# Softmax attention: maxima over 1024 keys in one pass, exponentials by single heads, the value product in one run a step

## The reference

```python
q = (x @ Wq).reshape(b, s, N_HEADS, D_K)
kk = (x @ Wk).reshape(b, s, N_KV, D_K)
v = (x @ Wv).reshape(b, s, N_KV, D_K)
...
scores = jnp.einsum('bqkgd,btkd->bkgqt', q, kk) * inv_sqrt_dk
attn = jax.nn.softmax(scores, axis=-1)
out = jnp.einsum('bkgqt,btkd->bqkgd', attn, v)
```

## Time and profile before

| | |
|---|---|
| time, median of 3 runs (lowest, highest) | 5175.65 us (5169.24, 5177.06) |
| the profiled execution: time, span | 5170.96 us, 5169.3 us |
| busy share of the span: TensorE, VectorE, ScalarE, GpSimd | 81%, 66%, 41%, 39% |
| granted TensorE clock, mean of the span | 0.916 |

### The profile page before, as it was taken

One profiled execution on the slowest core, in us unless ns is written; L12 is line 12 of the kernel. 1 busy time (PEld: TensorE's weight loads), 2 busy tenths in 40 slices (PEclk: granted clock), 3 DMA queues, 4 the chain that ended last, 5 costly groups with the idle time before them and its releaser, 6 DMA issues. The chain is left out here.

```text
span 5169.3 us, 79734 instructions
## 1 busy us (share of the span) xinstructions
PE 4208.5 (81%) x24362; PEld 2099.4 (41%) x24362; DVE 3391.5 (66%) x7610; ACT 2094.7 (41%) x3092; POOL 2028.3 (39%) x2141
## 2 busy tenths in 40 slices
PE   1548999999999999997588627787787797999999
PEld 0122333333333333333466514344344354666665
DVE  6838888888888888884455464454454555666665
ACT  1014555555555556555455402222222133333333
POOL 0300022212222222222344426656666663666665
PEclk9968999999999999998799858888888898999999
DMA  2951111111111111110322200000000001000000
GB/s 84 384 176 24 25 33 33 33 33 33 33 33 33 34 34 35 34 37 11 115 87 88 76 10 20 25 14 23 20 16 24 19 10 33 21 19 18 19 20 20
DMA packets 132918, 237.92 MB, mean 46 GB/s; under 512 B 27552, under 2 KB 32872, under 8 KB 132520
## 3 DMA queue, kind: packets, MB, share of 16 engines
q1 hardware_dynamic: 115656, 200.51, 14.5%
q0 software_dynamic: 16384, 33.59, 2.3%
q10 hardware_dynamic: 576, 0.02, 0.0%
HBM read 89.74 MB, written 144.31 MB: 45 GB/s over the span
## 5 line engine op out<-in xcount | busy, mean ns | idle before, releaser
L917 DVE TENSOR_REDUCE b_halfmax<-b_ps_m 128x1 f32<-128x512 f32 x2048 | 1342.0, 685 | 300.1 <-PE b_ps_m L1182 293.5
L1150 ACT ACTIVATE b_probs<-b_ps_s 128x1024 f32<-128x1024 f32 x1024 | 993.5, 1019 | 623.9 <-PE b_ps_s L1194 618.4
L1182 PE MATMUL b_ps_m<-b_ks,b_qs 96*128 96x512 bf16 x2048 | 827.7, 405 | 177.5 <-DVE b_halfmax L917 134.0
L1209 PE MATMUL b_ps_o<-b_probs,b_vs 128*32 128x256 f32 x8192 | 664.3, 401 | 0.6 <-ACT b_probs L1150 0.6
L1891 POOL TENSOR_TENSOR e_act_lo<-e_act,e_act_hi 128x512 fp32r<-128x512 f32 x384 | 519.2, 1352 | 348.7 <-DVE e_act_hi L1820 348.7
L1194 PE MATMUL b_ps_s<-b_qs,b_ks 99*128 99x512 bf16 x2048 | 632.7, 392 | 3.6 <-ACT b_probs L1150 3.3
L1182 PEld LDWEIGHTS b_ps_m<-b_ks,b_qs 96*128 96x128 bf16 x2048 | 202.7, 99 | 800.1 <-DVE b_halfmax L917 601.6
L2085 ACT ACTIVATE e_act<-e_ps_h,e_bias 128x512 f32<-128x512 f32 x384 | 263.8, 687 | 518.9 <-PE e_ps_h L2139 518.9
L1988 DVE TENSOR_TENSOR e_act<-e_act,e_ps_g 128x512 f32<-128x512 f32 x384 | 262.8, 685 | 292.4 <-ACT e_act L2085 289.4
L2512 POOL TENSOR_TENSOR d_q_wide<-d_raw,d_tab_q 128x512 f32<-128x512 f32 x256 | 321.5, 1277 | 110.0 <-ACT d_raw L2835 110.0
L2942 PE MATMUL d_ps_s<-d_q_wide,d_k_chan 128*128 128x512 f32 x512 | 307.0, 683 | 19.2 <-POOL d_q_wide L2512 19.2
(11 more groups left out here) (432 smaller groups left out, 7499.5 us busy)
## 6 DMA issues: line engine op xcount, KB each, us to landing
slots_out<-nothing SPq DMA_DIRECT2D x17, 4096.0 KB, 29.9
b_qs<-b_q_parts SPq DMA_DIRECT2D x96, 256.0 KB, 9.2
c_xin<-slots_in SPq DMA_DIRECT2D x71, 256.0 KB, 2.6
slots_out<-c_y_out SPq DMA_DIRECT2D x71, 256.0 KB, 2.0
b_q_parts<-b_qparts SPq DMA_DIRECT2D x16, 768.0 KB, 3.6
a_x<-in_x_dram SPq DMA_DIRECT2D x8, 1024.0 KB, 11.2
normalised_t<-d_xT SPq DMA_DIRECT2D x16, 512.0 KB, 2.6
e_xb<-normalised_t SPq DMA_DIRECT2D x32, 256.0 KB, 2.9
```

Of the source, the lines that this page charges most:

```text
L917: nc.vector.tensor_reduce(half_max[:, kv, u // 2, u % 2:u % 2 + 1], ps_m[:, u % 2, :], AX.X, ALU.max).then_inc(m_free, 1)
L1150: nc.scalar.activation(probs[:, s % 2, pair * 2 * HALF:(pair + 1) * 2 * HALF], ps_s[:, pair, :], ACT.Exp).then_inc(exp_done, 1)
L1182: nc.tensor.matmul(ps_m[:, u % 2, :], qs[0:STACK, buffer, h * PX + qt * P:h * PX + qt * P + P], ks[0:STACK, buffer, kv * PX + half * HALF: ...
L1209: last = nc.tensor.matmul(ps_o[32 * j:32 * j + 32, cols], vs[:, parity, tt, g // 2, :], probs[:, s % 2, j * HALF:(j + 1) * HALF][:, cols], ...
```

## The change

The four banks of scores and the two of maxima trade places. `ps_m` has two buffers of two banks: a unit of the maxima is now two matmuls over all 1024 keys and one reduce of 1024 elements straight into `maxes`; there are two units a step, and `whole_maxima` goes. `ps_s` has two buffers of one bank: a score matmul, its semaphore and its exponential are one head each. The value product is one run of four calls with 512 columns.

```diff
@@ -537,7 +537,7 @@
 
 MAX_FROM = 12
 MAX_HALF = 16
-MAX_PER_STEP = 2 * MAXES // MAX_HALF
+MAX_PER_STEP = MAXES // MAX_HALF
 STATS_AT, NORM_AT = 26, 29
...
@@ -578,8 +578,7 @@
         qs = sb("b_qs", [P, 2, HEADS * PX], BF16)
         ks = sb("b_ks", [P, 2, KV * PX], BF16)
         vs = sb("b_vs", [P, 2, TILES, KV, 2 * DK])
-        half_max = sb("b_halfmax", [P, KV, MAXES, 2])
-        maxes = sb("b_maxes", [P, MAXES])
+        maxes = sb("b_maxes", [P, KV, MAXES])
         m_parts = sb("b_mparts", [MAXES, 3, P], BF16)
         m_rest = sb("b_mrest", [MAXES, P])
...
@@ -606,8 +605,8 @@
         slot_f = sb("b_slot_f", [P, 2 * TILES])
         slot = sb("b_slot", [P, 2 * TILES], U32)
 
-        ps_s = ps("b_ps_s", [P, 2, 2 * HALF])
-        ps_m = ps("b_ps_m", [P, 2, HALF])
+        ps_s = ps("b_ps_s", [P, 2, HALF])
+        ps_m = ps("b_ps_m", [P, 2, PX])
         ps_o = ps("b_ps_o", [P, HALF])
         ps_x = ps("b_ps_x", [P, HALF])
...
@@ -912,10 +910,8 @@
                                       ).then_inc(part2_done, 1)
 
             def reduce_unit(m, kv, u):
-                wait_at = m * (4 * MAXES) + kv * 2 * MAXES + u
-                dve.wait_ge(m_ready, wait_at + 1)
-                nc.vector.tensor_reduce(half_max[:, kv, u // 2, u % 2:u % 2 + 1], ps_m[:, u % 2, :], AX.X,
-                                        ALU.max).then_inc(m_free, 1)
+                dve.wait_ge(m_ready, (2 * m + kv) * MAXES + u + 1)
+                nc.vector.tensor_reduce(maxes[:, kv, u:u + 1], ps_m[:, u % 2], AX.X, ALU.max).then_inc(m_free, 1)
 
...
@@ -1016,12 +1012,6 @@
                 dve.wait_ge(mp_step, g0 + 4)
                 nc.vector.tensor_copy(m_parts[:, 2, :], m_rest2[:]).then_inc(mp_step, 1)
 
-            def whole_maxima(m, kv):
-
-                dve.wait_ge(m_free, m * (4 * MAXES) + (kv + 1) * 2 * MAXES)
-                nc.vector.tensor_tensor(maxes[:], half_max[:, kv, :, 0], half_max[:, kv, :, 1],
-                                        ALU.max).then_inc(maxes_done, 1)
-
             def read_out(n, name):
                 m = n + 1
...
@@ -1045,11 +1035,11 @@
                     statistics(0, 0, 1)
                 for s in range(STEPS):
                     units = max_units(n, s)
-                    for unit in units[:2]:
+                    for unit in units[:1]:
                         reduce_unit(*unit)
                     for name in filled_at(n, s - 1):
                         read_out(n, name)
-                    for unit in units[2:]:
+                    for unit in units[1:]:
                         reduce_unit(*unit)
                     if s in (STATS2_AT, STATS2_AT + 1) and finish:
                         statistics(n - 1, 1, s - STATS2_AT)
@@ -1059,10 +1049,6 @@
                         gate_weights(n)
                     if s == SLOTS_AT and finish:
                         slots_of(n - 1)
-                    if s == MAX_FROM - 1 and steps:
-                        whole_maxima(n, 1)
-                    if s == MAX_FROM + MAX_HALF - 1 and prepare:
-                        whole_maxima(m, 0)
                     if steps and s and s % TILES == 0:
                         out_of(n, s // TILES - 1)
...
@@ -1143,13 +1129,11 @@
                         act.wait_ge(g_step, 7 * (n - 1) + 3)
                         nc.scalar.activation(expo[:], gap[:], ACT.Exp).then_inc(gap_exp, 1)
                     if steps:
-                        for pair in range(2):
-                            v = 2 * s + pair
-                            act.wait_ge(s_ready, 2 * STEPS * n + v + 1)
+                        for j in range(GROUP):
+                            act.wait_ge(s_ready, GROUP * (STEPS * n + s) + j + 1)
                             positive(act, pv_done, STEPS * n + s - 1)
-                            nc.scalar.activation(
-                                probs[:, s % 2, pair * 2 * HALF:(pair + 1) * 2 * HALF], ps_s[:, pair, :],
-                                ACT.Exp).then_inc(exp_done, 1)
+                            nc.scalar.activation(probs[:, s % 2, j * HALF:(j + 1) * HALF], ps_s[:, j % 2], ACT.Exp
+                                                 ).then_inc(exp_done, 1)
 
             act.wait_ge(const, 11)
...
@@ -1177,41 +1161,38 @@
                                  start=True, stop=True).then_inc(x_ready, 1)
 
             def max_unit(m, kv, u, buffer):
-                h, qt, half = kv * GROUP + u // 2 // TILES, u // 2 % TILES, u % 2
-                positive(pe, m_free, m * (4 * MAXES) + kv * 2 * MAXES + u - 1)
-                nc.tensor.matmul(
-                    ps_m[:, u % 2, :], qs[0:STACK, buffer, h * PX + qt * P:h * PX + qt * P + P],
-                    ks[0:STACK, buffer, kv * PX + half * HALF:kv * PX + half * HALF + HALF],
-                    start=True, stop=True).then_inc(m_ready, 1)
-
-            def scores(n, s, parity, pair):
+                h, qt = kv * GROUP + u // TILES, u % TILES
+                positive(pe, m_free, (2 * m + kv) * MAXES + u - 1)
+                for half in range(2):
+                    last = nc.tensor.matmul(
+                        ps_m[:, u % 2, half * HALF:(half + 1) * HALF],
+                        qs[0:STACK, buffer, h * PX + qt * P:h * PX + qt * P + P],
+                        ks[0:STACK, buffer, kv * PX + half * HALF:kv * PX + half * HALF + HALF],
+                        start=True, stop=True)
+                last.then_inc(m_ready, 1)
+
+            def scores(n, s, parity, j):
                 g, tt = s // TILES, s % TILES
                 kv, half = g // 2, g % 2
-                rows = STACK + 3
-                positive(pe, exp_done, 2 * STEPS * n + 2 * s + pair - 1)
-                for j in range(2):
-                    h = kv * GROUP + 2 * pair + j
-                    last = nc.tensor.matmul(
-                        ps_s[:, pair, j * HALF:(j + 1) * HALF],
-                        ks[0:rows, parity, kv * PX + tt * P:kv * PX + tt * P + P],
-                        qs[0:rows, parity, h * PX + half * HALF:h * PX + half * HALF + HALF],
-                        start=True, stop=True)
-                last.then_inc(s_ready, 1)
-
-            def products(n, s, parity, part):
-
-                cols = slice(part * HALF // 2, (part + 1) * HALF // 2)
+                rows, h = STACK + 3, kv * GROUP + j
+                positive(pe, exp_done, GROUP * (STEPS * n + s) + j - 1)
+                nc.tensor.matmul(
+                    ps_s[:, j % 2], ks[0:rows, parity, kv * PX + tt * P:kv * PX + tt * P + P],
+                    qs[0:rows, parity, h * PX + half * HALF:h * PX + half * HALF + HALF],
+                    start=True, stop=True).then_inc(s_ready, 1)
+
+            def products(n, s, parity):
+
                 g, tt = s // TILES, s % TILES
-                pe.wait_ge(exp_done, 2 * STEPS * n + 2 * s + 2)
-                if tt == 0 and part == 0:
+                pe.wait_ge(exp_done, GROUP * (STEPS * n + s) + GROUP)
+                if tt == 0:
                     positive(pe, o_free, 4 * n + g)
                 for j in range(GROUP):
                     last = nc.tensor.matmul(
-                        ps_o[32 * j:32 * j + 32, cols], vs[:, parity, tt, g // 2, :],
-                        probs[:, s % 2, j * HALF:(j + 1) * HALF][:, cols],
-                        start=(tt == 0 and part == 0), stop=(tt == TILES - 1), skip_group_check=True)
-                if part:
-                    last.then_inc(pv_done, 1)
+                        ps_o[32 * j:32 * j + 32, :], vs[:, parity, tt, g // 2, :],
+                        probs[:, s % 2, j * HALF:(j + 1) * HALF],
+                        start=(tt == 0), stop=(tt == TILES - 1), skip_group_check=True)
+                last.then_inc(pv_done, 1)
 
...
@@ -1257,8 +1238,9 @@
                     last.then_inc(x_ready, 1)
                 else:
                     fill(n, name)
-                    wait_apart(pe, maxes_done, 2 * n + 2 if name == "mt1" else 2 * m + 1, passed)
-                    nc.tensor.transpose(ps_x[0:MAXES, 0:P], maxes[:], ident[:]).then_inc(x_ready, 1)
+                    image, kv = (n, 1) if name == "mt1" else (m, 0)
+                    wait_apart(pe, m_free, (2 * image + kv + 1) * MAXES, passed)
+                    nc.tensor.transpose(ps_x[0:MAXES, 0:P], maxes[:, kv], ident[:]).then_inc(x_ready, 1)
 
             def body(n, parity):
...
@@ -1274,16 +1256,14 @@
 
                     buffer = 1 - parity if s >= MAX_FROM else parity
                     between = [unit + (buffer,) for unit in max_units(n, s)] if s < STEPS else []
-                    for pair in range(2 if steps and s < STEPS else 0):
-                        for unit in between[:1]:
-                            max_unit(*unit)
-                        del between[:1]
-                        scores(n, s, parity, pair)
-                    for part in range(2 if steps and s else 0):
-                        for unit in between[:1]:
-                            max_unit(*unit)
```

(13 more changed lines are left out.)

## The result

| | before | after |
|---|---|---|
| median of 13 runs each (lowest, highest) | 5175.65 us (5168.76, 5184.82) | 5191.97 us (5183.6, 5207.53) |
| the profiled execution: time, span | 5170.96, 5169.3 us | 5187.78, 5186.1 us |

The ratio is 1.0032, with a 95% interval of 1.0024 to 1.0039: slower by 16 us, a little more than such a measurement tells from no change. The forecast was 5178 in a range of 5133 to 5235.

A forecast was written before the change was run, and what follows sets the result against it. TensorE was taken to bound the kernel, with VectorE close behind. The terms -54 + 50 - 3 + 14 = +7, set against the profiled 5170.96 us, gave 5178, in a range of 5133 to 5235.

The forecast's parts named there:

- the steps without the clock: 15 images with maxima for the next: -3.6 us an image, together -54, counting no time at half clock.
- the clock: Half clock behind stalls at normalising and gate: two to three falls an image, 2.4 x 1.4 x 15 = +50 us.
- image 0's maxima: Making image 0's maxima: 64 reduces' savings of 0.03 to 0.07 each, -3 us.
- the last image: 20 steps without maxima, where head 2's wait is less covered: 2.62 us a step against 2.05, +14 us.
- Where the bound lies: Attention stage: TensorE bounds, busy 1760.2 of 1906.0 us; VectorE close behind, ScalarE with room.
- The value product in one run: Product in each step: 1.01 us in one piece; TensorE's own work falls from 3.08 to about 2.85.
- Scores and exponentials by one head: Head 2's scores wait for head 0's exponential: round trip 1.08 us, plain step 3.05 against 3.08.
- The rival in which it comes back in time: Exponential's round trip below 1.05 us: 5142 with half the wait gone, 5106 with all; chance 0.20.
- the rival of 3.12 a step: Signals or exponential cost more in plain steps: +34 us, 5212, up to 5225 with two full reduces; chance 0.12.
- Maxima over 1024 keys: Two VectorE reduces a step for four, 1.16 us each, saving 0.06 to 0.15 a step; buffers hold a whole step.
- The sum by groups: One image's steps: 1-9 +0.2, 18-19 -2.4, 20-25 -0.6, 26-30 -1.4, 10-14 +0.4, rest +0.2; together -3.6 us.
- The clock as a rival: Short waits and stalls bring two more half-clock falls an image, +42: 5220 us; decides above three an image; chance 0.18.

The follow-up runs named there:

- The halves: Changed kernel with the value product in two halves of 256 columns directly behind each other, eight calls for four: 5198.48 us, 1.0055 of before.
- The two banks in the kernel before: Kernel before with only scores and exponentials by one head, in two one-bank buffers: 5463.25 us, 1.0564 of before.
- the new order: Changed kernel with all four maxima matmuls of a step between heads 1 and 2 on TensorE: 5179.96 us, 1.0014 of before.
- the order of its neighbours' work fitted to it: Changed kernel with maxima matmuls between heads 1 and 2, normalising behind the exponentials, gate read behind both maxima: 5059.08 us, 0.9778 of before.
- the two that could be tried in the kernel before: Kernel before with normalising behind the exponentials and the gate read behind all four maxima of step 18: 5174.17 us, 1.0004 of before.
- the late normalising: Changed kernel with ScalarE's normalising moved behind the exponentials of its step: 5086.63 us, 0.9836 of before.
- the kernel with the order and the late normalising: Changed kernel with maxima matmuls between heads 1 and 2 and normalising behind the exponentials: 5086.93 us, 0.9831 of before.

## Why the prediction held, and where its terms were off

**The number.** It lay within the range, with some luck. The sum is +7 and the profiled execution gave +16.8. The forecast set its +7 against the profiled execution of before, 4.7 below the median, so as a median it should have read 5183. The terms differ by -26 (the steps without the clock), +35 (the clock), -7 (image 0's maxima), +5 (the last image) and +3 (later stages): the two largest errors nearly cancel.

**Where the bound lies.** Right. The 15 images took 1911.1 us; the sum had 1906 - 54 + 50 = 1902.

**The value product in one run.** Right: 1.00 from its start to the next matmul (1523.69 to 1524.69), for 1.01. The halves showed that the gain is that of the two changes of kind saved in each step. The kernel with that part alone showed something the term didn't say: in its order the gain is lost without the deeper buffers of the maxima.

**Scores and exponentials by one head.** The plain step of 3.05 was met, with the round trip of 1.08. The two banks in the kernel before and the new order, 2.88 without the wait, show from both sides that the round trip sets it. The exponential took 0.595, for 0.60. The rival in which it comes back in time fell with that, and so did the rival of 3.12 a step.

**Maxima over 1024 keys.** The reduce takes 1.217 alone; two in a row take 2.34 and three 3.45, so one occupies 1.11, for 1.16. The idle time that the reduce ends fell to 27.5 us, below the 50 named. Making image 0's maxima was mis-sized: the first exponential came at 408.4 and not at 418.6, 10 us earlier where 3 stood. The term counted only what the reduces save. The rest comes with this part of the change: with the heads in two or in four banks, or the product in one run, in the kernel before, the first exponential still came at 417.2, 419.0 and 416.6. The deeper buffers are its likely cause, since VectorE is busy there for 49.54 of 51.00 us, at a granted clock of 0.50; no run has them without the longer reduce.

**The sum by groups.** Without the clock it held: 18 and 19 took 7.48 (7.4), 20 to 25 18.67 (18.4), 1 to 9 38.85 (38.6). Steps 10 to 14 took 22.25 and 26 to 30 20.79, for 19.8 and 19.5; the half-clock stretches in them had TensorE busy for 6.02 and 3.41 us, which at the full clock would be half of that, so 19.2 and 19.1 are left. The stalls were 3.09 and 3.06, where "nearly 3 us" stood. The clock's price falls on the steps behind the stalls, and the sum had it in a line of its own.

**The clock.** This is the term that was mis-sized most: +50 was too small. The 15 images have 40 stretches at half clock, for 36 counted, 2.7 an image; TensorE is busy in them for 170.1 us, which costs up to 85 us, 2.1 each where 1.4 was taken. (In the kernel before it is 32 stretches with 137.7 us busy.) The -54 was too small as well: 1911.1 - 85 is 1826, and the sum without the clock had 1852. The two errors, +35 and -26, nearly cancel, and that is luck. The size of a fall was taken from a single one that lasted 3.41 us, and the one in steps 10 to 14 lasted 6.84. The mean clock came out at 0.95, the lower end of what was named.

**The clock as a rival.** By its own sign it did not decide: not more than three falls an image. But most of its price came, +35 of the +42, by longer falls and not by more of them. Its mechanism is refuted for the short waits of plain steps, by row: in each of steps 20 to 25 a score matmul starts 0.21 late, and their clock is 1.00. Most falls stand behind single long stalls, 3.09, 3.06 or 2.02; the six in step 18 do not. The Trainium skill (TensorE: Matmul & The Clock Gate, A second HAM failure mode) tells of matmul groups that cycle through PSUM and idle briefly between them, and of a clock that swings. The plain steps of this kernel do not agree, nor do steps 20 to 25 of the kernel with two banks, where the wait is 0.70 a step and the clock is 1.00 in all 15 images. In its steps 7, 17 and 18, which have fills, 14 falls begin with no idle piece over 0.5 us in the 7 us before; what those stand behind is open.

**The last image.** +14 was taken and +19 measured; part of that is the clock, since it has 13.7 us at half clock up to its last exponential, for 3.4 before. It takes 143.7 us from 2319.5 to the end of the stage at 2463.2, for 124.7 before. The plain step here is 2.88, not 2.62 (the next one starts at 2396.54):

```profile
2393.66 0.60 PE L1179 MATMUL b_ps_s<-b_qs,b_ks 99*128 99x512 bf16 x2
2394.74 0.88 PE L1179 MATMUL b_ps_s<-b_qs,b_ks 99*128 99x512 bf16 x2 [0.47 <-ACT b_probs L1135]
2395.54 1.06 PE L1191 MATMUL b_ps_o<-b_probs,b_vs 128*32 128x512 f32 x8
```

Head 2 starts 1.08 after head 0, as worked out. But head 3 waits as well (0.88 for two matmuls, for 0.60): its buffer is freed by head 1's exponential, and ScalarE spends 0.50 on each. The step that failed is "1.08 + 0.22 + 0.31 + 1.01", whose 0.22 has to be 0.50. In steps with maxima two of their matmuls stand there, so the error touched only the last image.

**What stays open.** The later stages took 3 us more (2722.8 for 2719.9 from the end of the attention stage). The experiments don't touch them either, and in ten of the eleven they took 2719.7 to 2726.5 (2738.4 in the other), so this says nothing of the change.

## What to carry to other kernels

Before a PSUM buffer is split, add up its round trip (matmul, signal, reading instruction, signal: 1.08 us here for 512 columns) and hold it against the work that stands between two uses of the buffer in the instruction list; what is left over is paid in every step. Shallower buffers also turn things that used to be hidden into stalls: look at what the reading engine does ahead of the critical instruction (here 1.65 us of normalising behind a 2.9 us wait for another engine) and move it behind. The change alone made this kernel 0.3% slower; with the order of its neighbours' work fitted to it, it is 2.2% faster than before, and of those edits the two that could be tried in the kernel before did nothing there. Price a stall with the clock behind it: of the 95 us that the late normalising took from the 15 images, about 67 are the clock's by the estimate above.

## What the runs showed of the hardware

- In the changed kernel each of 33 stalls of TensorE of 2.9 to 3.4 us was met by 3.4 or 6.8 us at a granted clock of 0.50, and none of eight of 0.7 to 1.6 us was. Of the eleven stalls of 2.0 to 2.1 us in the kernel with the order and the late normalising six were. A score matmul that starts 0.21 late in each step of 3.05 us leaves the clock at 1.00. Taking the stalls of 3.1 us away brought the mean clock of the stage from 0.95 to 0.99.
- Where a product (fp32, four groups of 32 columns) follows bf16 matmuls, 0.31 passes to its start for the 0.22 between two bf16 matmuls, both before and after the change; 16 records of 256 columns or 8 of 512 take the same 1.00.
- A reduce of 1024 elements over two PSUM banks occupies 1.11 us, less than twice the 0.61 that one of 512 occupies.
